# One sum for a chunk of x, both turned halves on ScalarE and one Newton chain for two in the steps without tiles

## The chip, the core and the metric

The kernel runs on one core of a Trainium2 chip. The metric is device microseconds from launch to end, as the median of several runs.

## The reference, cut to what matters

`x` is (64, 12, 224, 224). Each 16x16 patch is summed, and twelve channels are mixed into a 192 wide token. A layer of attention with a polynomial in place of the exponential follows, then a mixture of eight experts of which each token takes two.

```python
pooled = x.reshape(Bb, Cc, n, K, n, K).sum(axis=(3, 5))
h = jnp.einsum('bcij,ce->bije', pooled, channel_weights).reshape(Bb, n * n, EMBED)
h = h + attn(layernorm(h), w_qkv, w_proj, b_proj)      # attn = relu(1 + qk + qk^2/2), normalised
h = h + ffn(layernorm(h), router_w, w1, b1, w2, b2)    # top 2 of 8 experts, exact gelu
# layernorm(x) = (x - mean) / sqrt(var + 1e-5)
```

## The kernel before, in words

The 64 images go through in 16 **steps** of four images. A step has 8 blocks of 98 tokens. Its x (9.6 MB) comes in 14 **chunks** of 672 KB into seven slots of `xbuf`; each chunk is two **halves**, and a half is summed by one VectorE instruction (`P`, L1069: 21 sums of 32 numbers on each partition). After each half `s_pooled` rises by one, and SyncE reloads the slot when both halves are summed (`P` of SyncE, L490, load L469).

The work of a step has stages, each with a part on several engines. Step s+1 is pooled while step s is in its later stages:

- **S1** (in steps without tiles `T1`): TensorE mixes the sums of the next step (L866), which needs all 28 halves.
- **S2** (in steps without tiles `T2`, L1171, for step s+1): VectorE reads the mixed channels and their variance, takes 1/sqrt of it with `inverse_root` (L1127: a first guess and three Newton rounds of three instructions, each of which waits for the one before) and builds the products `phi`.
- **S3**: TensorE makes moments (L876) and turns `phi` (L802); ScalarE copies `gts` (L680) and `phiT` (L682). **S4** and **S5**: two more products (L888, L898) with ScalarE copies between them (L686, L692, L693). **S6**: TensorE makes the numerators in four quarters (L909), VectorE divides each (`rden` L1183, `att` L1185).
- **S7**: TensorE turns `att` in four pieces, the upper and the lower half of the channels for each of two groups of images (L802). ScalarE copies the upper half to `attA` (L697), VectorE the lower one to `attB` (L1190).
- **S8**: TensorE multiplies (L933 from `attA`, L934 from `attB`) in four quarters, ScalarE copies `h1s` (L705), VectorE takes statistics and the top 8 of the router (L1197, L1198).
- **S10**: VectorE gathers mean and variance `var2`, the indices of the two best and the mask. **R** (L1219): a second `inverse_root` for the rows of the experts, then `shift2` (L1222) and `gap` (L1224). **V**: ScalarE takes a tanh of `gap` (L712) and normalises the rows (L716), in its queue ahead of S3 of the next step.
- **S11**, **S9**: VectorE finishes the gates and the slots (L1230 to L1255). **Q**: GpSimd scatters the rows with 16 indirect DMAs (L608). S11 and V wait until the rows of the step before have landed.

Who does what when is written out by hand: `tiles_do` (L403) walks a list of names, and each engine runs its own handler for each name in that order. Steps 0, 1 and 2 have the list `STEP_ALONE` (L159), step 3 has `LAST` (L169), in which the first experts' tiles are prepared (G0 to G5). Those four are the steps without tiles. Steps 4 to 15 (`ORDER`) carry three tiles of 512 rows of the experts each, and a tail of tiles follows. `P` takes the halves in order, so the place of each in the list is its number:

```python
STEP_ALONE = """S3 P P P P P P P P P P P P P P P P S4 S5 P P S6.0 S6.1 P S6.2 P S6.3 S7.0 P P S7.1 P P S8.0 P S8.1 P S8.2 P P S8.3
    T1 S10 T2 R V.0 V.1 S11 V.2 V.3 S9 Q0 Q1 Q2 Q3""".split()
LAST = """S3 P P P P P P P P P P S4 S5 P P P G0 G4 S6.0 S6.1 S6.2 S6.3 S7.0 P S7.1 P P G5 G1 P S8.0 S8.1 S8.2 S8.3 S10
    R V.0 S11 V.1 V.2 S9 V.3 Q0 Q1 Q2 Q3 P P P G2 P P P P G3 P P P P""".split()
```

`mark` and `own` (L1048, L1053) count the links of VectorE's own chain; each step has 44, and the count has to come out the same whichever list is run. Seven halves of step 1 are summed in the setup (`n_early`).

Of the kernel before, what the change touches and what calls it, by code (L numbers as in the profile page):

```python
# [181 lines left out]
def vit_layer(nc, x, cw, w_qkv, w_proj, b_proj, router, w1, b1, w2, b2, consts, padids, out):  # L182
# [3 lines left out]
    with ExitStack() as ctx:  # L186
# [27 lines left out]
        var1 = sb("var1", [TOK, NT])  # L214
        rstd1 = sb("rstd1", [TOK, NT])
        newton = sb("newton", [TOK, 2, NT])
# [12 lines left out]
        var2 = sb("var2", [TOK, NT])  # L229
        rstd2 = sb("rstd2", [TOK, NT])  # L230
# [139 lines left out]
        rank_bank, lone = [2], [False]  # L370
# [214 lines left out]
        def _(pool):  # L585
# [8 lines left out]
            given("pool", "fills", nc.gpsimd.memset(rstd1[:], 1.0))  # L594
# [58 lines left out]
        def _(act):  # L653
# [388 lines left out]
        def _(dve):  # L1042
# [3 lines left out]
            pos_ = {k: 0 for k in links}  # L1046

            def mark(ins, kind="step"):  # L1048

                pos_[kind] += 1  # L1050
                return ins.then_inc(own_sem[kind], 1)
# [10 lines left out]
            def P(s, p, first=False):  # L1062
# [64 lines left out]
            def inverse_root(s, y, v):  # L1127


# [3 lines left out]
                for _ in range(3):  # L1133
                    mark(V.tensor_tensor(newton[:, 0], y, y, ALU.mult))
                    own(s)
                    mark(V.scalar_tensor_tensor(out=newton[:, 1], in0=newton[:, 0], scalar=-0.5, in1=v,
                                                op0=ALU.mult, op1=ALU.mult))
                    own(s)
                    mark(V.scalar_tensor_tensor(out=y, in0=newton[:, 1], scalar=1.5, in1=y,
                                                op0=ALU.add, op1=ALU.mult))  # L1140
                    own(s)
# [3 lines left out]
            def S2(s, round=None):  # L1145
# [11 lines left out]
                mark(V.tensor_reduce(var1[:], prod[:], AX.X, ALU.add))  # L1157
                own(round)
                mark(V.tensor_scalar(var1[:], var1[:], EPS, None, ALU.add))
                own(round)  # L1160
                inverse_root(round, rstd1[:], var1[:])
                mark(V.tensor_tensor(phi[:, :, 1:U], att_ch, bc(rstd1[:], C), ALU.mult))
# [8 lines left out]
            def T2(s):  # L1171

                before = pos_["step"]
                S2(s + 1, s)
# [26 lines left out]
            def S10(s):  # L1201
# [7 lines left out]
                V.tensor_scalar(var2[:].unsqueeze(2), mv[:, :, 1:2], EPS, None, ALU.add)  # L1209
# [9 lines left out]
            def R(s):  # L1219

                inverse_root(s, rstd2[:], var2[:])
                V.scalar_tensor_tensor(out=shift2[:].unsqueeze(2), in0=mv[:, :, 0:1], scalar=-1.0,  # L1222
                                       in1=rstd2[:].unsqueeze(2), op0=ALU.mult, op1=ALU.mult)
                V.tensor_tensor(gap[:], gap[:], rstd2[:], ALU.mult).then_inc(s_gap, 1)  # L1224
# [158 lines left out]
            def P_left(s, p):  # L1383
                if after_first(s) or p >= n_early[0]:
# [43 lines left out]
```

## Time and profile before

| | |
|---|---|
| median of 3 runs | 1357.04 us (1356.02 to 1359.77) |
| profiled execution | span 1353.8 us from its first to its last instruction; what lies outside the span is not recorded apart |
| busy | PE 91%, DVE 71%, ACT 44%, POOL 44% of the span |
| setup | 0 to about 63 us |
| steps without tiles | about 63 to 231 us |
| steps with tiles | about 231 to 1050 us |
| tail of tiles | to the end |

The page of the profile gives busy shares for the whole span and, in forty slices, when each engine was busy. The stages differ, so each is read by itself: timelines of single engines, where each line has the start, the duration, the engine, the source line, the operation and what it writes and reads, and in brackets the idle time ahead of it with what ended that.

### The profile page before, as it was taken

What the parts mean: (1) busy time and instruction counts of PE and PEld (TensorE: products, weight loads), DVE (VectorE), ACT (ScalarE), POOL (GpSimd) and SP (SyncE); (2) the same over time, 40 slices, a digit from 0 to 9 for tenths busy, and PEclk for the clock granted to TensorE, in tenths of its full rate; (3) what the DMA queues carried; (4) which work ended last, traced back from release to release, by engine and by line L of the source; (5) the groups of instructions that cost most, each with busy time, mean ns of one, the idle gap of its engine ahead of it and who ended that gap; (6) DMA issues with size and microseconds to landing.
All of it is one profiled execution on the core that took longest, in us unless ns stands there. A gap on an engine that the chain in (4) does not pass through costs nothing.

```text
span 1353.8 us, 26903 instructions
## 1 busy us (share of the span) xinstructions
PE 1228.0 (91%) x7299; PEld 1093.9 (81%) x7299; DVE 956.8 (71%) x3407; ACT 596.2 (44%) x1127; POOL 600.4 (44%) x483
## 2 busy tenths in 40 slices
PE   5867766999999999899999899999999979999997
PEld 3756655888888888788888788888888879998996
DVE  6799998787878787877787687868783523333454
ACT  1221223454545454445444354535454534544664
POOL 0104333425454454453644545464555464533433
PEclk9986556999999999898999899989999989999999
DMA  9679887767878887778786878877744655544555
GB/s 354 231 254 347 320 281 262 231 220 240 238 232 221 255 216 245 204 238 218 234 246 217 210 237 234 250 208 234 195 129 80 211 117 130 107 95 89 119 142 112
DMA packets 126551, 284.42 MB, mean 210 GB/s; under 512 B 24819, under 2 KB 70500, under 8 KB 126500
## 3 DMA queue, kind: packets, MB, share of 16 engines
q1 hardware_dynamic: 82762, 241.95, 54.5%
q0 software_dynamic: 43104, 41.25, 17.7%
q10 hardware_dynamic: 634, 0.61, 0.2%
q8 instruction: 23, 0.38, 0.1%
q14 instruction: 28, 0.23, 0.0%
HBM read 228.79 MB, written 54.95 MB: 210 GB/s over the span
## 4 chain that ended last, share of the span: by engine, by line
PE 33%; DMA 19%; DVE 17%; POOL 15%; issue 14%; ACT 1%; POOLq 1%; SPq 0%; ACTq 0%; DVEq 0%
PE ps L993 11%; DMA result<-ys,ridx 11%; PE ps L962 10%; POOL rows_d L608 8%; DMA rows_d<-rows,sloti 7%; POOL result L623 7%; DVE red L1069 6%; PE ps L802 3%; PE ps L933 2%; PE ps L934 2%; DMA w1r<-L_attn_w_qkv 1%; DVE stats L1197 1%; DVE topi L1206 1%; PE ps L1022 1%; DMA xr<-rows_d 1%
## 5 line engine op out<-in xcount | busy, mean ns | idle before, releaser
L623 POOL DMA_INDIRECT result<-ys,ridx x210 | 333.1, 1586 | 307.9 <-issue 120.4
L993 PE MATMUL ps<-w2a,hid 128*128 x2520 | 455.5, 327 | 0.0
L608 POOL DMA_INDIRECT rows_d<-rows,sloti x256 | 258.9, 1011 | 394.0 <-DMA rows_d<-rows,sloti 146.7
L993 PEld LDWEIGHTS ps<-w2a,hid 128*128 128x128 f32 x2520 | 415.4, 190 | 11.8 <-issue 0.2
L1069 DVE TENSOR_REDUCE red<-xbuf 128x21 f32<-128x672 f32 x448 | 359.2, 841 | 5.3 <-PE ps L866 2.4
L727 ACT ACTIVATE hid<-ps,b1s 128x512 f32<-128x512 f32 (+1 forms) x344 | 222.9, 654 | 239.2 <-PE ps L962 230.5
L962 PE MATMUL ps<-xh,w1h 128*128 128x512 f32 (+1 forms) x344 | 166.0, 482 | 7.9 <-DVE xl L1306 3.9
L1329 DVE TENSOR_TENSOR w1l<-w1r,w1h 128x768 fp32r<-128x768 f32 x116 | 110.3, 951 | 70.9 <-ACT w1h L739 70.3
L962 PE MATMUL ps<-xh,w1l 128*128 128x512 f32 (+1 forms) x344 | 131.5, 382 | 0.0
L962 PE MATMUL ps<-xb,w1h 128*128 128x512 f32 (+1 forms) x344 | 131.3, 382 | 0.0
L962 PE MATMUL ps<-xl,w1h 128*128 128x512 f32 (+1 forms) x344 | 131.2, 381 | 0.0
L962 PE MATMUL ps<-xb,w1l 128*128 128x512 f32 (+1 forms) x344 | 130.8, 380 | 0.0
L739 ACT CAST w1h<-w1r 128x768 fp32r<-128x768 f32 x116 | 96.2, 830 | 28.4 <-PE ps L962 28.1
L760 ACT ACTIVATE ys<-ps,gate 128x192 f32<-128x192 f32 x210 | 71.7, 423 | 73.9 <-PE ps L993 73.7
L1306 DVE TENSOR_TENSOR xl<-ps,xh 128x512 fp32r<-128x512 f32 (+1 forms) x58 | 37.1, 639 | 88.8 <-ACT xh L746 88.6
L802 PE MATMUL ps<-cst,xr 128*128 128x128 f32 (+1 forms) x428 | 67.3, 277 | 22.0 <-DMA xr<-rows_d 14.4
L962 PEld LDWEIGHTS ps<-xh,w1h 128*128 128x128 f32 x344 | 66.3, 193 | 22.2 <-issue 6.9
L746 ACT CAST xh<-ps 128x512 fp32r<-128x512 f32 (+1 forms) x58 | 31.8, 548 | 107.6 <-PE ps L802 107.5
L802 PEld LDWEIGHTS ps<-cst,xr 128*128 128x128 f32 (+1 forms) x428 | 53.8, 143 | 30.8 <-DMA xr<-rows_d 14.3
L962 PEld LDWEIGHTS ps<-xb,w1l 128*128 128x128 f32 x344 | 65.6, 191 | 13.4
L962 PEld LDWEIGHTS ps<-xh,w1l 128*128 128x128 f32 x344 | 65.8, 191 | 13.0
L962 PEld LDWEIGHTS ps<-xb,w1h 128*128 128x128 f32 x344 | 65.8, 191 | 13.1
(164 smaller groups left out, 1633.8 us busy)
## 6 DMA issues: line engine op xcount, KB each, us to landing
xbuf<-x SPq DMA_DIRECT2D x224, 672.0 KB, 5.6
w1r<-L_ffn_w SPq DMA_DIRECT2D x118, 384.0 KB, 3.7
xr<-rows_d SPq DMA_DIRECT2D x48, 402.0 KB, 3.4
result<-h1s SPq DMA_DIRECT2D x32, 294.0 KB
w2a<-L_ffn_w SPq DMA_DIRECT2D x8, 576.0 KB, 7.6
rows_d<-rows,sloti POOLq DMA_INDIRECT x256
rows_d<-pad SPq DMA_DIRECT2D x9, 402.0 KB, 4.6
result<-ys,ridx POOLq DMA_INDIRECT x210, 4.9
```

The costliest lines, as they stand in the source:

```text
L608: pool.indirect_dma_start(rows_d, bass.IndirectOffsetOnAxis(ap=sloti[:, k * NT + t:k * NT + t + 1], axis=0), rows[:, t, :], None).then_inc ...
L623: pool.indirect_dma_start(out, bass.IndirectOffsetOnAxis(ap=ridx[:, b, n:n + 1], axis=0), ys[:, b, n, :], None, compute_op=ALU.add).then_i ...
L727: nc.scalar.activation(hid[:, m % 3, 0:128 * g], ps[:, bank(b, f"M{m}"), 0:128 * g], ACT.Gelu, bias=b1s[:, b, m:m + 1]).then_inc(s_hT, 1)
L739: copy(w1h[:, :, cols], w1r[:, nb, q]).then_inc(s_w1h, 1)
L746: copy(xh[:, nb, 0:128 * g], ps[:, bank(b, "X0"), 0:128 * g]).then_inc(s_xa, 1)
L760: nc.scalar.activation(ys[:, b, i, :], yout(g, b, i), ACT.Copy, scale=gate[:, b, i:i + 1]).then_inc(s_ys, TP // g)
L802: return nc.tensor.transpose(dst, src, ident[0:n, 0:n])
L962: last = mm(ps[:, bank(b, f"M{m}"), 0:128 * g], w, r, start=i == 0, stop=i == len(parts) - 1)
L993: last = mm(yout(g, b, n), hid[:, m % 3, cols], w, start=False, stop=m == MC - 1 and n % 2 == 1)
L1069: V.tensor_reduce(red[:, p * SUMS:(p + 1) * SUMS], xbuf[:, k % XSLOTS, h], AX.X, ALU.add).then_inc(s_pooled, 1)
L1306: V.tensor_tensor(xl[:, nb, 0:128 * g], ps[:, bank(b, "X0"), 0:128 * g], xh[:, nb, 0:128 * g].bitcast(F32), ALU.subtract).then_inc(s_xd, 1)
L1329: V.tensor_tensor(w1l[:, :, cols], w1r[:, nb, q], w1h[:, :, cols].bitcast(F32), ALU.subtract).then_inc(s_w1l, 1)
```

## The change

It has three parts, all for the steps without tiles.

1. `P` gets a form `whole`: one VectorE instruction sums both halves of a chunk (42 sums of 32 numbers) and raises `s_pooled` by two. It stands where the even half stood, and the odd half's place stays empty. This holds for the halves from 8 on in step 0 and for all in steps 1 to 3.
2. In S7 the copy of `attB` goes from VectorE to ScalarE, behind the copy of `attA` of the same group. VectorE keeps its wait for the turn.
3. `var1` and `var2`, `rstd1` and `rstd2` lie side by side. In steps 0 to 2 `T2` takes both roots at once, with ten instructions of 16 columns instead of 8, and `R` has no chain of its own; it raises the counter of the links by ten. Step 3 and the steps with tiles keep two chains.

```diff
             lone[0] = not with_tiles and not last
+            early[0] = not with_tiles
...
                 copy(attA[:, g * IPS * TOK:(g + 1) * IPS * TOK],
                      ps[0:KA, TURN[2 * g], 0:IPS * TOK]).then_inc(s_tA, 1)
+                if early[0]:
+                    act.wait_ge(s_turn, s * 4 + 2 * g + 2)
+                    copy(attB[:, g * IPS * TOK:(g + 1) * IPS * TOK],
+                         ps[0:KB, TURN[2 * g + 1], 0:IPS * TOK]).then_inc(s_tB, 1)
...
-                V.tensor_reduce(red[:, p * SUMS:(p + 1) * SUMS], xbuf[:, k % XSLOTS, h], AX.X,
-                                ALU.add).then_inc(s_pooled, 1)
+                if whole:
+                    V.tensor_reduce(red[:, p * SUMS:(p + HALVES) * SUMS].rearrange("p (h n) -> p h n", h=HALVES),
+                                    xbuf[:, k % XSLOTS], AX.X, ALU.add).then_inc(s_pooled, HALVES)
+                else:
+                    V.tensor_reduce(red[:, p * SUMS:(p + 1) * SUMS], xbuf[:, k % XSLOTS, h], AX.X,
+                                    ALU.add).then_inc(s_pooled, 1)
...
-            def inverse_root(s, y, v):
+            def inverse_root(s, which):
+                y = roots[:, which].rearrange("p k t -> p (k t)")
+                v = vars_[:, which].rearrange("p k t -> p (k t)")
...
-                inverse_root(round, rstd1[:], var1[:])
+                inverse_root(round, slice(0, 2) if both else slice(0, 1))
...
-                S2(s + 1, s)
+                S2(s + 1, s, both=True)
...
                 dve.wait_ge(s_turn, s * 4 + 2 * g + 2)
+                if early[0]:
+                    return
                 V.tensor_copy(attB[:, g * IPS * TOK:(g + 1) * IPS * TOK],
...
             def R(s):
-                inverse_root(s, rstd2[:], var2[:])
+                if not lone[0]:
+                    inverse_root(s, slice(1, 2))
...
+                if lone[0]:
+                    mark(shifts, n=ROOT)
...
             def P_left(s, p):
-                if after_first(s) or p >= n_early[0]:
+                if early[0] and (after_first(s) or p > n_early[0]):
+                    if p % HALVES == 0:
+                        P(s, p, whole=True)
+                elif after_first(s) or p >= n_early[0]:
                     P(s, p)
```

## Rows read from the trace of the kernel before

**Rows 1.** The page: busy time and share of the span of each engine.

```profile
PE 1228.0 (91%) x7299; PEld 1093.9 (81%) x7299; DVE 956.8 (71%) x3407; ACT 596.2 (44%) x1127; POOL 600.4 (44%) x483
```

**Rows 2.** Windows: start:end, length, busy of five engines, PE clock, DMA share, GB/s.

```profile
95.50:137.20 41.70, 28.58 (x141) 24.51 (x141) 38.94 (x134) 9.43 (x20) 15.26 (x16) 0.58 0.84 306
137.20:180.20 43.00, 29.53 (x141) 25.26 (x141) 38.98 (x133) 9.43 (x20) 15.20 (x16) 0.58 0.85 308
...
240.00:1000.00 760.00, 728.65 (x4392) 648.54 (x4392) 603.80 (x2120) 365.70 (x676) 371.09 (x296) 0.98 0.79 226
...
600.00:640.00 40.00, 38.15 (x209) 34.23 (x209) 28.17 (x107) 18.61 (x38) 19.09 (x13) 0.91 0.84 221
```

**Rows 3.** Groups of VectorE from 95 to 236 us: count, busy us, mean ns.

```profile
L1069 DVE TENSOR_REDUCE red<-xbuf 128x21 f32<-128x672 f32 x84 | 65.6, 843 | 0.3 <-issue 0.3
...
L1157 DVE TENSOR_REDUCE var<-prod 98x8 f32<-98x96 f32 x3 | 0.8, 253 | 0.1
```

**Rows 4.** Timeline of VectorE, second root of step 0 to its pooling.

```profile
95.48 0.16 DVE L1131 TENSOR_SCALAR rstd<-var 98x8 int32<-98x8 int32 x1
...
97.48 0.17 DVE L1222 SCALAR_TENSOR_TENSOR shift<-mv,rstd 98x8 f32<-98x8 f32 x1
...
100.01 13.77 DVE L1069 TENSOR_REDUCE red<-xbuf 128x21 f32<-128x672 f32 x18
```

**Rows 5.** Timeline of ScalarE in step 1.

```profile
97.87 3.60 ACT L716 ACTIVATE rows<-h1s,shift,rstd 98x192 f32<-98x192 f32 x8
...
101.72 0.80 ACT L682 COPY phiT<-ps 91x784 f32<-91x784 f32 x1
...
119.82 0.49 ACT L697 COPY attA<-ps 103x392 f32<-103x392 f32 x1 [1.35 <-PE ps L802]
```

**Rows 6.** Timeline of TensorE in step 1.

```profile
98.16 1.61 PE L802 MATMUL ps<-cst,phi 98*91 98x98 f32 x8
...
111.51 5.76 PE L909 MATMUL ps<-us,phiT 91*98 91x204 f32 x16 [0.98 <-ACT us L693]
...
118.77 1.66 PE L802 MATMUL ps<-cst,att 98*103 98x98 f32 x8 [0.17 <-DVE att L1185]
120.23 0.88 PE L933 MATMUL ps<-resA,attA 103*98 103x200 f32 x2
```

**Rows 7.** Timeline of VectorE in step 1, from the numerators to the statistics.

```profile
113.69 0.30 DVE L1183 RECIPROCAL rden<-ps 98x24 f32<-98x24 f32 x1
...
120.64 0.56 DVE L1190 COPY attB<-ps 102x392 f32<-102x392 f32 x1
121.11 1.60 DVE L1069 TENSOR_REDUCE red<-xbuf 128x21 f32<-128x672 f32 x2
123.69 0.36 DVE L1197 BATCH_NORM_STATS2 stats<-h1s 98x6 f32<-98x192 f32 x1 [0.98 <-ACT h1s L705]
```

**Rows 8.** Timeline of TensorE in step 2.

```profile
160.74 1.66 PE L802 MATMUL ps<-cst,att 98*103 98x98 f32 x8 [0.44 <-DVE att L1185]
162.20 0.88 PE L933 MATMUL ps<-resA,attA 103*98 103x200 f32 x2
...
166.86 0.71 PE L934 MATMUL ps<-resB,attB 102*98 102x200 f32 x2
167.41 0.50 PE L933 MATMUL ps<-resA,attA 103*98 103x200 f32 x2
```

**Rows 9.** Timeline of VectorE in step 3.

```profile
212.88 0.36 DVE L1197 BATCH_NORM_STATS2 stats<-h1s 98x6 f32<-98x192 f32 x1 [0.60 <-ACT h1s L705]
...
220.93 2.36 DVE L1069 TENSOR_REDUCE red<-xbuf 128x21 f32<-128x672 f32 x3
223.21 0.68 DVE L1306 TENSOR_TENSOR xl<-ps,xh 128x512 fp32r<-128x512 f32 x1
...
225.04 6.16 DVE L1069 TENSOR_REDUCE red<-xbuf 128x21 f32<-128x672 f32 x8
```

**Rows 10.** Timelines at the end of step 3: ScalarE's `xh`, TensorE's S1.

```profile
222.46 0.59 ACT L746 CAST xh<-ps 128x512 fp32r<-128x512 f32 x1
...
231.25 1.51 PE L866 MATMUL ps<-mixg,red 128*98 128x96 f32 x12 [1.94 <-DVE red L1069]
```

**Rows 11.** Timelines of GpSimd and VectorE around the scatter of step 0.

```profile
131.34 0.95 POOL L608 DMA_INDIRECT rows_d<-rows,sloti  x1 [0.30 <-issue]
...
139.35 0.17 DVE L1230 CAST rows<-ids 98x8 int32<-98x8 f32 x1
```

More of the change, by code:

```diff
@@ L213, in vit_layer @@
         prod = sb("prod", [TOK, NT, C])
-        var1 = sb("var1", [TOK, NT])
-        rstd1 = sb("rstd1", [TOK, NT])
-        newton = sb("newton", [TOK, 2, NT])
+        vars_ = sb("vars", [TOK, 2, NT])
+        roots = sb("roots", [TOK, 2, NT])
+        var1, var2 = vars_[:, 0], vars_[:, 1]
+        rstd1, rstd2 = roots[:, 0], roots[:, 1]
+        newton = sb("newton", [TOK, 2, 2 * NT])
         phi = sb("phi", [TOK, NT, NF])
@@ L369, in vit_layer @@
         at_end = [False]
-        rank_bank, lone = [2], [False]
+        rank_bank, lone, early = [2], [False], [False]
         def groups(j):
@@ L593, in _ @@
             nc.gpsimd.memset(b2t[:], 0.0)
-            given("pool", "fills", nc.gpsimd.memset(rstd1[:], 1.0))
+            given("pool", "fills", nc.gpsimd.memset(roots[:], 1.0))
             pool.wait_ge(d_w, 16 * 9)
@@ L1046, in _, with mark @@
             pos_ = {k: 0 for k in links}
-            def mark(ins, kind="step"):
-                pos_[kind] += 1
-                return ins.then_inc(own_sem[kind], 1)
+            ROOT = 10
+            def mark(ins, kind="step", n=1):
+                pos_[kind] += n
+                return ins.then_inc(own_sem[kind], n)
             def own(i, kind="step", alone=False):
@@ L1060, in bc, with P @@
                 return ap.unsqueeze(len(ap.shape)).to_broadcast(list(ap.shape) + [n])
-            def P(s, p, first=False):
+            def P(s, p, first=False, whole=False):
                 k, h = p // HALVES, p % HALVES
@@ L1125, in _ @@
             given("dve", "b2", V.tensor_copy(b2s[:, 2], b2f[:, 0]))
-            def inverse_root(s, y, v):
+            def inverse_root(s, which):
+                y = roots[:, which].rearrange("p k t -> p (k t)")
+                v = vars_[:, which].rearrange("p k t -> p (k t)")
+                n = y.shape[1]
+                squares, halves = newton[:, 0, 0:n], newton[:, 1, 0:n]
                 mark(V.tensor_scalar(y.bitcast(I32), v.bitcast(I32), -0.5, float(0x5f3759df), ALU.mult, ALU.add))
@@ L1133, in inverse_root @@
                 for _ in range(3):
-                    mark(V.tensor_tensor(newton[:, 0], y, y, ALU.mult))
+                    mark(V.tensor_tensor(squares, y, y, ALU.mult))
                     own(s)
-                    mark(V.scalar_tensor_tensor(out=newton[:, 1], in0=newton[:, 0], scalar=-0.5, in1=v,
+                    mark(V.scalar_tensor_tensor(out=halves, in0=squares, scalar=-0.5, in1=v,
                                                 op0=ALU.mult, op1=ALU.mult))
                     own(s)
-                    mark(V.scalar_tensor_tensor(out=y, in0=newton[:, 1], scalar=1.5, in1=y,
+                    mark(V.scalar_tensor_tensor(out=y, in0=halves, scalar=1.5, in1=y,
                                                 op0=ALU.add, op1=ALU.mult))
@@ L1219, in R @@
             def R(s):
-                inverse_root(s, rstd2[:], var2[:])
-                V.scalar_tensor_tensor(out=shift2[:].unsqueeze(2), in0=mv[:, :, 0:1], scalar=-1.0,
-                                       in1=rstd2[:].unsqueeze(2), op0=ALU.mult, op1=ALU.mult)
-                V.tensor_tensor(gap[:], gap[:], rstd2[:], ALU.mult).then_inc(s_gap, 1)
+                if not lone[0]:
+                    inverse_root(s, slice(1, 2))
+                shifts = V.scalar_tensor_tensor(out=shift2[:].unsqueeze(2), in0=mv[:, :, 0:1], scalar=-1.0,
+                                                in1=rstd2.unsqueeze(2), op0=ALU.mult, op1=ALU.mult)
+                if lone[0]:
+                    mark(shifts, n=ROOT)
+                V.tensor_tensor(gap[:], gap[:], rstd2, ALU.mult).then_inc(s_gap, 1)
             def S11(s):
```

12 lines of the change are left out of this document (5 added, 7 removed).

## The prediction

> **What bounds the kernel now.** I begin with the page. TensorE is busy 91% of the span and VectorE 71% [rows 1], which would say that an edit of VectorE's work is worth little. The windows say otherwise of the stage that the edit touches. In steps 1 and 2 VectorE is busy 38.9 of 41.7 and 39.0 of 43.0 us and TensorE, at a mean clock of 0.58, only 28.6 and 29.5; from 240 to 1000 us TensorE is busy 728.65 of 760 us [rows 2]. So the steps with tiles go at TensorE's pace and the steps without tiles at a loop that runs mostly through VectorE. What is saved there moves all that follows to the left.
>
> The loop is read in the timelines of step 1. VectorE ends `phi`, and behind it stands the second root, from 95.48 to the start of `shift2` at 97.48 [rows 4]. Only then can ScalarE take the tanh and normalise rows, 97.87 plus 3.60, and behind these in its queue are the copies of S3 for the next step, `phiT` at 101.72 [rows 5], although TensorE has turned it by 98.16 + 1.61 = 99.77 [rows 6]. S4, S5 and the numerators (111.51) hang on that. At the same time VectorE sums 18 halves, 100.01 to 113.78 [rows 4], and comes to the first numerator at 113.69 [rows 7]; the first quarter of the sixteen products that take 5.76 us is ready at 111.51 + 1.44 = 112.95 [rows 6]. The two arms of the loop, VectorE's pooling and the ScalarE/TensorE arm, thus differ by 0.7 us only. After the numerators TensorE and ScalarE lead: VectorE idles 0.98 us for `h1s` [rows 7].
>
> **The change part by part.**
>
> *The joined root.* The second chain goes: 97.48 − 95.48 = 2.00 us [rows 4], in three steps. The joined chain has 8 more columns in ten instructions. The slope of VectorE's sums is (843 − 253)/(672 − 96) = 1.02 ns for a column [rows 3], so 80 ns more ahead of `phi`. On VectorE's arm pooling starts 2.0 us sooner after `phi`. On the other arm rows are normalised 2.0 us sooner and end at 97.87 + 3.60 − 2.0 = 99.47; `phiT` could then start at 99.8, and TensorE has turned it at 99.77, so nearly all of the 2.0 arrives; I take 1.9. Net 1.9 − 0.1 = 1.8 a step, **5.4 us** in three. What is late next on this arm is TensorE's turn of `phi`, 0.1 us behind: a longer cut would have been lost there. In step 3 `R` keeps its chain, so nothing there.
>
> *The whole chunk.* Eighteen halves take 13.77 us with the last of 0.84 running out, so (13.77 − 0.84)/17 = 0.76 us from one to the next [rows 4]. 672 columns at 1.02 ns are 0.69, which leaves about 0.07 us for each instruction. One of 1344 columns doesn't occur in the trace. Its bounds are 1.52 us (nothing saved) and 1.37 (no fixed part at all); I take 2 x 0.76 − 0.07 = 1.45, since a single instruction keeps one fixed part, and rows of either length lie on that line. There are 10 such pairs in step 0 and 14 in each of three, 52 x 0.07 = 3.6 us of VectorE. On the path is little of it. The 9 chunks ahead of the numerators bring VectorE's arm 2.0 + 0.6 us forward where the other comes 1.9 forward; with its slack of 0.7 the other arm then decides, just. Between S8.0 and S8.3 there are two chunks, 0.14 us in each of three steps, **0.4 us**. In step 3 half 17 moves ahead of S8.0 and costs nothing: 0.7 us more there against 0.5 from the copy that has gone and 0.6 of idle time at the last `h1s` [rows 9]. Behind S9 there were 3 + 8 halves, and now 1 + 4 chunks. The three give way to one (1.45 for 2.28), but `xl` then waits for `xh`, which ended at 223.05 [rows 10] against 223.21 [rows 9], so 0.1 is won and not 0.8; the eight give 4 x 0.07 = 0.3. **0.4 us**. TensorE's mix starts 0.1 us behind the last sum, at 231.25 [rows 10], and releases the steps with tiles.
>
> The places move too. In S6 the chunk stands whole between the second and third quarter, so the third `att` is 0.7 us later and the fourth 0.07 earlier. TensorE still has the fourth numerator and the first turns to do until then. It costs nothing while the numerators' 5.76 us end after that, which holds in steps 1 and 2. SyncE reloads a slot when a chunk's second half is done, which is 0.07 us sooner or earlier still; no load waits longer, and in the stage VectorE idled 0.3 us in all ahead of its sums, none of it for a load [rows 3].
>
> *The copies on ScalarE.* VectorE loses two `attB` copies a step, 121.11 − 120.64 = 0.47 us each [rows 7], 3.8 us in four steps. I cost this at nothing: behind them VectorE idles 0.98 us for `h1s` [rows 7], and will idle some 2 us. ScalarE gets two copies of 392 columns; the nearest row is `attA` with 0.49 us, and it idled 1.35 us ahead of that [rows 5]. Behind the copy of `attB` of group 0 stands only `attA` of group 1, which S8.1 needs 2.7 us after S8.0 starts. In step 3 ScalarE's casts of `w1` come 0.4 us later, ahead of a `w1l` that VectorE reaches 0.5 us sooner; the slack up to `h1s` is over 1 us. Cover gone, a copy costs 0.4 to 0.5 us a step.
> The Trainium skill speaks against this part: "Trainium Architecture — The Big Picture", "The five engines, in one table", says that ScalarE is not for simple arithmetic and that VectorE is up to about three times faster for each element. The rows of the same width read 0.49 us on ScalarE and 0.56 on VectorE [rows 5, 7], so they don't bear it out for a copy from PSUM. At three times, an estimate from that page, a copy would take 1.5 us and the second one of a group would reach into S8.1, at about 1 us a step.
>
> *Gaps closed.* TensorE waited 0.17 us in step 1 and 0.44 in step 2 for the fourth `att` [rows 6, 8]. VectorE's arm comes forward by 2.6 and the other by 1.9, so these go: **0.6 us**.
>
> *A landing.* S11 and V of step 1 wait until the rows of step 0 have landed. Their last indirect DMA starts at 131.34, and VectorE passes the wait at 139.35 [rows 11]. Between them lie 8.0 us, 0.95 for the DMA's issue and the rest for its landing and what margin there is. The scatter starts 2.0 us sooner, the wait comes 2.0 + 1.8 sooner (the cuts of steps 0 and 1), so the margin shrinks by 1.8. Bounds 0 and 1 us; I take 0.1, as step 2's margin is larger.
>
> *The clock.* TensorE runs these stages at half clock until deep in S8: the products come every 0.67 us and every 0.34 after the rise to 2.4 GHz. In step 2 seven pairs are slow (162.20 to 166.86) [rows 8]; in step 1 the rise comes after four. The engine had then worked nearly without a gap from the numerators on. If the rise keeps its time while the products start 2 us sooner, three more pairs are slow, and VectorE's chunk between the quarters hides about half of it; if it comes earlier in step 2, 0.9 us of idle time go. Bounds −1 and +2 us over the stage, in my sum 0.
>
> Sum: 5.4 + 0.4 + 0.4 + 0.6 − 0.1 = 6.7 us. The span of the profiled execution would go from 1353.8 to 1347.1; it is 3.2 us under the median of the runs, and the same offset gives 1357.0 − 6.7 = **1350.3 us**. It passes through if the steps with tiles take the shift whole. They do the same instructions in the same order on the same data, so nothing in the code holds them to a time.
>
> **The rivals.**
> 1. *The gain is cut or given back.* TensorE at half clock keeps the slow pairs (1 us), S11 waits for the landing (1 us), and an S6 or S7 order gives 0.5 us a step; or the steps with tiles lose a little. For it: the two arms are only 0.7 us apart and a third, TensorE's turn, 0.1 us. Against: each single part is small. Half the gain, 3.4 us: 1353.6. Chance 0.2.
> 2. *VectorE alone sets the stage.* Then all its work counts: 3 x 1.9 + 3.6 + 3.8 = 13.1 us, 1343.9. For it its 93%; against it the 0.98 us for `h1s` [rows 7]. Chance 0.03.
> 3. *Slower.* The mechanism is TensorE's clock in the steps with tiles. The stretch from 600 to 640 us has a mean clock of 0.91 [rows 2], which is 7.2 us at 1.2 GHz and up to 3.6 us of work not done in them; such a fall stands in few of the stretches, since from 240 to 1000 us the mean is 0.98, about four falls' worth. Shifted arrivals can put a short wait of TensorE where it lets the clock fall. From two more falls on (2 x 3.6 = 7.2) the gain is gone; with three more, one in every fourth of the twelve steps with tiles, the time is 1350.3 + 10.8 = 1361.1. Chance 0.04. The Trainium skill ("TensorE: Matmul & The Clock Gate", "Part 1: The HAM clock gate") says that the engine is slow by default and that activity releases it, by which a fall needs TensorE to idle; the stretches with 0.91 do have less work done. It would leave this chance as low as it is.
> 4. *It doesn't do what it says.* The instruction of 1344 columns takes as long as two. Then the 0.4 + 0.3 go and the pooling arm comes 2.0 forward, still ahead of the other: 1351.1, inside the forecast.
>
> **How the numbers follow.** Forecast 0.72, rivals 0.2, 0.03 and 0.04, and 0.01 for the rest. The forecast with its bounds is 1348 to 1352.5 (clock, landing, chunk). Runs of one kernel spread over 3.7 us. To hold 8 in 10 the range reaches into rival 1 and a little towards rival 2: 1346.5 to 1354.5. A measurement can tell from no change about 0.3%, that is 4.1 us, so faster means under 1352.9. That holds in nearly all of the forecast, in rival 2 and in a quarter of rival 1: 0.76. Same 0.19, slower 0.05.
>
> **What would show it.** From the end of `phi` to the next, steps 1 and 2 take 41.7 and 43.0 us; I expect about 39.7 and 40.7, and step 0 hardly changed. ScalarE's `rows` start 0.4 us after `phi`, not 2.4. The chunk's instruction has a duration near 1.53 us and follows its like every 1.45. VectorE's idle time ahead of the first statistics grows from 1 to about 2 us, which is where the copies went. TensorE's mix of step 4 starts near 224.5, not 231.25. From there on the timelines should be the old ones, shifted. I am wrong if `phi` to `phi` shrinks by under 1.3 us (an arm that I took for slack decides), or by over 3, or if the distance from TensorE's mix of step 4 to the end, 1122 us, changes by more than 2 us.

## The result and the profile after

| | before | after |
|---|---|---|
| median of 13 runs each | 1356.76 us (1352.57 to 1363.85) | 1365.01 us (1357.17 to 1367.87) |
| ratio to before, 95% interval | | 1.005 [1.0032, 1.0068] |
| profiled span | 1353.8 us | 1363.5 us (its execution took 1365.31) |
| mix of step 4 starts | 231.25 us | 227.58 us |
| from there to the mix of step 15 | 771.8 us | 786.6 us |
| from there to the end | 350.7 us | 349.4 us |

The change makes the kernel 0.5% slower where I forecast 0.5% faster. (The ratios here and below are of undisturbed runs of both kernels on one chip, and so can differ a little from the quotient of the medians.) The last three lines of the table split the span: the part that was edited gained 3.7 us, the part in which nothing was edited lost 14.8, and the tail gained 1.3. Sum +9.8 by the rounded numbers, against 9.7 in the spans.

First the page, busy time of each engine and the queue that fetches instructions, whose columns are packets, MB and share. The first line answers [rows 1].

```profile
PE 1238.0 (91%) x7299; PEld 1098.3 (81%) x7299; DVE 945.8 (69%) x3317; ACT 600.4 (44%) x1135; POOL 598.9 (44%) x483
...
q14 instruction: 78, 0.64, 0.1%
```

VectorE did 11 us less. The line of the queue read `q14 instruction: 28, 0.23, 0.0%` before: fifty packets more. That is a row of which I had made nothing.

Next the windows, for [rows 2] (a step's slow stage, and the steps with tiles).

```profile
100.00:140.00 40.00, 28.65 (x136) 24.55 (x137) 34.86 (x106) 9.44 (x21) 14.35 (x16) 0.59 0.91 332
...
240.00:1000.00 760.00, 720.91 (x4297) 637.51 (x4296) 589.63 (x2070) 355.13 (x657) 364.53 (x288) 0.97 0.78 225
```

In the same 760 us TensorE got 7.7 us less done. To compare equal work (4455 products in both) I take the windows from the mix of step 4 to the mix of step 15, before and after:

```profile
231.25:1003.07 771.82, 740.47 (x4455) 659.23 (x4456) 612.78 (x2157) 368.00 (x681) 376.53 (x300) 0.98 0.78 226
227.58:1014.14 786.56, 746.78 (x4455) 660.52 (x4456) 612.22 (x2157) 368.23 (x681) 377.16 (x300) 0.97 0.76 223
```

Of the 14.8 us TensorE is idle for 8.4 more (31.4 and 39.8) and busy 6.3 more for the same products. The two clocks are 0.976 and 0.974 to a third digit, which is under 2 us of it; I have no cause for the rest of the busy time. The idle time by itself proves little, since the kernel with all parts undone, below, idles 39.6 us there too. What TensorE waited for, from 240 to 1000 us (who waited for whom, us in total, times, longest):

```profile
PE ps L967 <- DVE xl L1325: 19.6, 17, 1.8
PE ps L881 <- DVE phi L1179: 7.7, 10, 1.8
```

The trace of before has no wait of TensorE for `phi` in these steps; its longest sum is 18.6 us for `att`, which is 4.8 after. So the waits moved, and one in every turn is new. And `phi` is made late because VectorE stands still ahead of it. Its waits from 240 to 1040 us:

```profile
DVE rden L1197 <- PE ps L914: 54.9, 12, 6.4
DVE vars L1173 <- issue: 30.7, 10, 4.2
DVE xl L1325 <- ACT xh L751: 24.3, 11, 2.2
DVE avail L1283 <- issue: 14.1, 10, 2.0
```

"Issue" is time in which the engine waited for nothing that the profile shows. The trace of before has neither of the two rows. Both are in ten turns, once a turn, of the loop of the steps with tiles. (The loop is walked eleven times, for steps 4 to 14, so VectorE jumps back ten times.) Here is one turn's start, VectorE's timeline, after:

```profile
368.97 0.17 DVE L1283 COPY avail<-base 128x8 f32<-128x8 f32 x1 [1.02 <-issue]
369.78 0.26 DVE L1166 COPY att<-ps 98x96 f32<-98x96 f32 x1 [0.63 <-PE ps L871]
370.07 0.25 DVE L1168 TENSOR_TENSOR prod<-att,ps 98x96 f32<-98x96 f32 x1
370.36 0.25 DVE L1171 TENSOR_REDUCE vars<-prod 98x8 f32<-98x96 f32 x1
373.29 0.17 DVE L1173 TENSOR_SCALAR vars<-vars 98x8 f32<-98x8 f32 x1 [2.68 <-issue]
```

and the same place before:

```profile
367.21 0.15 DVE L1264 COPY avail<-base 128x8 f32<-128x8 f32 x1
369.09 0.26 DVE L1152 COPY att<-ps 98x96 f32<-98x96 f32 x1 [1.74 <-PE ps L866]
369.38 0.25 DVE L1154 TENSOR_TENSOR prod<-att,ps 98x96 f32<-98x96 f32 x1
369.67 0.25 DVE L1157 TENSOR_REDUCE var<-prod 98x8 f32<-98x96 f32 x1
369.96 0.17 DVE L1159 TENSOR_SCALAR var<-var 98x8 f32<-98x8 f32 x1
```

Before, the step ahead of the root follows its predecessor at once. After, VectorE stands still for 2.7 us between two instructions of a few hundred nanoseconds of which the second needs only the first. One turn of the steps with tiles is one pass of a loop in VectorE's code, and `avail` is the first instruction behind the jump to its start, where the other 1.0 us of idle time lies, there still partly hidden by the wait for the mix.

Last the steps without tiles, VectorE and ScalarE from the second root of step 0 on, for [rows 4, 5, 7]:

```profile
95.70 0.16 DVE L1239 SCALAR_TENSOR_TENSOR shift<-mv,roots 98x8 f32<-98x8 f32 x1
...
98.29 13.23 DVE L1076 TENSOR_REDUCE red<-xbuf 128x42 f32<-128x1344 f32 x9
111.54 0.31 DVE L1197 RECIPROCAL rden<-ps 98x24 f32<-98x24 f32 x1
...
122.08 0.36 DVE L1213 BATCH_NORM_STATS2 stats<-h1s 98x6 f32<-98x192 f32 x1 [1.64 <-ACT h1s L710]
```

```profile
96.08 3.60 ACT L721 ACTIVATE rows<-h1s,shift,roots 98x192 f32<-98x192 f32 x8
100.03 0.81 ACT L683 COPY phiT<-ps 91x784 f32<-91x784 f32 x1
...
117.05 0.49 ACT L702 COPY attB<-ps 102x392 f32<-102x392 f32 x1 [0.27 <-PE ps L807]
118.83 0.49 ACT L702 COPY attB<-ps 102x392 f32<-102x392 f32 x1 [0.17 <-PE ps L807]
```

and TensorE's products of step 1, for [rows 6]:

```profile
118.58 0.88 PE L938 MATMUL ps<-resA,attA 103*98 103x200 f32 x2
...
122.58 0.88 PE L938 MATMUL ps<-resA,attA 103*98 103x200 f32 x2
123.25 0.78 PE L939 MATMUL ps<-resB,attB 102*98 102x200 f32 x2
```

`rows` starts 1.8 us sooner, the numerators' first division 2.1 sooner, the products 1.65 sooner. All of this came as worked out. But the mix of step 2 (L871) starts at 128.22 instead of 128.84: from 87.39, step 1 took 40.8 us instead of 41.6, and the next two 41.0 for 43.0 and 58.4 for 59.4. TensorE waited for VectorE's sums ahead of that mix both times.

### The profile page after: what moved, and what is told of

Its sections match the earlier page's. It is cut to its first block, busy times and chain, and to the rows that moved or that the text cites. A ratio compares the mean times of both kernels' runs of the same rounds, so it can differ in the third digit from the quotient of the medians.

```text
span 1363.5 us, 26853 instructions
## 1 busy us (share of the span) xinstructions
PE 1238.0 (91%) x7299; PEld 1098.3 (81%) x7299; DVE 945.8 (69%) x3317; ACT 600.4 (44%) x1135; POOL 598.9 (44%) x483
## 4 chain that ended last, share of the span: by engine, by line
PE 49%; DVE 32%; issue 12%; ACT 3%; DMA 2%; POOL 1%; DVEq 0%; ACTq 0%; POOLq 0%; SPq 0%
PE ps L998 17%; PE ps L967 16%; DVE red L1079 8%; PE ps L807 3%; PE ps L903 2%; PE ps L893 2%; DVE stats L1213 2%; PE ps L914 2%; DVE w1l L1348 2%; DVE red L1076 2%; DVE phi L1179 2%; DVE topi L1222 1%; PE ps L938 1%; PE ps L939 1%; DVE xl L1325 1%
## 5 line engine op out<-in xcount | busy, mean ns | idle before, releaser
L998 PE MATMUL ps<-w2a,hid 128*128 x2520 | 463.1, 331 | 0.0
L998 PEld LDWEIGHTS ps<-w2a,hid 128*128 128x128 f32 x2520 | 423.4, 194 | 12.4 <-issue 0.2
L1079 DVE TENSOR_REDUCE red<-xbuf 128x21 f32<-128x672 f32 x344 | 277.7, 841 | 5.0 <-PE ps L871 2.4
L1076 DVE TENSOR_REDUCE red<-xbuf 128x42 f32<-128x1344 f32 x52 | 77.8, 1543 | 3.2 <-PE ps L807 2.6
L967 PEld LDWEIGHTS ps<-xb,w1l 128*128 128x128 f32 x344 | 65.9, 192 | 13.4
```

The lines of the kernel that those rows point to most:

```text
L967: last = mm(ps[:, bank(b, f"M{m}"), 0:128 * g], w, r, start=i == 0, stop=i == len(parts) - 1)
L998: last = mm(yout(g, b, n), hid[:, m % 3, cols], w, start=False, stop=m == MC - 1 and n % 2 == 1)
L1076: V.tensor_reduce(red[:, p * SUMS:(p + HALVES) * SUMS].rearrange("p (h n) -> p h n", h=HALVES), xbuf[:, k % XSLOTS], AX.X, ALU.add).then_i ...
```

## The experiments

**The theory** after the traces: it is the place of the loop in VectorE's code. The list of instructions ahead of the loop of the steps with tiles was 36 shorter (541 instead of 577 in the built programs), while the loop itself kept its length. If code is fetched in blocks, the loop begins at another place of a block, covers one more, and is fetched anew in every turn. **The rival**: the work in the steps with tiles arrives shifted by 3.7 us against x and the experts' DMAs and the tiles' order, and loses by that. A second one is that a part of the change does harm by what it computes.

The tool for all of them is padding that does nothing: increments of a semaphore on VectorE, put where it idles about 5 us at the start of the program for its first load.

```diff
+            for _ in range(36):
+                dve.sem_inc(s_waits, 1)
             dve.wait_ge(d_cst, 16)
```

**The change with 36, 12 and 4 increments in front.** With 36 the loop is where it was before.

> The changed kernel with 36 short semaphore instructions put in front of VectorE's stream, where it idles 5 us for its first load. VectorE's list before the loop of the steps with tiles is 36 instructions shorter in the changed kernel; this gives the loop its old place. Theory P (the place of the loop in VectorE's instruction stream makes it refetch code each turn): the idle time of VectorE without a releaser at the start of each step with tiles (30.7 + 14.1 us in all) goes, the instruction packets between 320 and 960 us go from some 50 to none, and the time is 1352.5 +- 2.5, 12 us under the changed kernel. Theory C (the earlier start shifts the phase of TensorE's clock and of the DMA queues in the loop): nothing of it goes, 1363 to 1366.

> The same with 12 instructions. The stall of the changed kernel stands about 11 instructions behind the start of the loop, so by theory P the border of a block of code lies there; 12 more in front move the loop's start over the border and the loop lies in one block less: no stalls, 1352.5 +- 2.5, as with 36. Theory C: 1363 to 1366. If only the exact old place were good, this one would be as slow as the changed kernel.

> The same with 4 instructions. By theory P the border is now about 7 instructions behind the loop's start instead of 11: the stall moves from ahead of L1173 to ahead of the TENSOR_TENSOR prod (L1168) or the reduce L1171 behind it, its size stays near 3 us a step and the time stays near 1363. Theory C has no stall that moves with the count; 1363 to 1366 too. So the place of the stall decides, not the time.

**The kernel before with 220.** Here none of the change's parts is in the code.

> The kernel before with 220 such instructions in front, 256 less the 36, which puts the loop where the changed kernel has it if code is fetched in blocks of 256 instructions. Nothing else is changed; up to 3 us may be lost at the start. Theory P: VectorE's idle time without a releaser appears (some 4 us a step), about 50 more instruction packets, and from TensorE's mix of step 4 to that of step 15 the time grows from 772 to about 786 us; in all 1367 to 1372. Theory C: the distance stays near 772 and the time at 1357 to 1360.

| on one chip, before 1356.83 us | median us | ratio [95%] | mix of step 4 | mix 4 to mix 15 | q14 packets |
|---|---|---|---|---|---|
| change + 36 | 1352.81 | 0.9969 [0.9943, 0.9994] | 227.55 | 771.7 | 28 |
| change + 12 | 1349.77 | 0.9955 [0.9928, 0.9982] | 227.37 | 764.8 | 28 |
| change + 4 | 1370.57 | 1.0101 [1.0072, 1.013] | 227.83 | 792.6 | 78 |
| before + 220 | 1386.33 | 1.0226 [1.0199, 1.0254] | 244.86 | 785.5 | 80 |

The shift against the DMAs is the same in the first three (227.4 to 227.8), and the loss is there in one and gone in two. That ends the first rival. The distance itself scatters: in one profile each it is 762 to 776 us in the twelve kernels without the extra packets and 778 to 802 in the six with them. The two ranges don't touch, but a difference of a few us within one of them means nothing. The timeline of VectorE at the loop's start, with 12 and then with 4:

```profile
362.04 0.15 DVE L1285 COPY avail<-base 128x8 f32<-128x8 f32 x1
363.94 0.26 DVE L1168 COPY att<-ps 98x96 f32<-98x96 f32 x1 [1.75 <-PE ps L871]
```

```profile
366.61 0.17 DVE L1285 COPY avail<-base 128x8 f32<-128x8 f32 x1 [1.22 <-issue]
367.21 0.26 DVE L1168 COPY att<-ps 98x96 f32<-98x96 f32 x1 [0.42 <-PE ps L871]
370.47 0.25 DVE L1170 TENSOR_TENSOR prod<-att,ps 98x96 f32<-98x96 f32 x1 [3.00 <-issue]
```

With four more instructions in front the second stall comes earlier in the turn, ahead of `prod` and no longer ahead of the step behind `vars`, as a fixed border in the code requires. In the kernel before with 220 it stands ahead of `var` again, and the distance is 785.5 us: the loss is there without the change. Its start was a miss. I expected up to 3 us for the 220, but VectorE's first instruction starts at 21.99 us and not at 5.15, and the mix of step 4 comes 13.6 us later. Up to 36 of them are hidden (5.22).

**The parts alone**, each also a place of its own. In the built programs the chunk alone takes one instruction away ahead of the loop, since a wait stays where each sum or copy was; the copies alone take one too, the joined root alone takes 30, and all three together take 36. In the first kernel R keeps its chain and `attB` is copied by VectorE, in the second sums are by halves and R keeps its chain, in the third sums are by halves and VectorE copies `attB`; the fourth is the third with 30 increments.

```diff
# chunk alone, and copies alone
-                S2(s + 1, s, both=True)
+                S2(s + 1, s)
# copies alone, and root alone
-                if early[0] and (after_first(s) or p > n_early[0]):
+                if False:
```

> Only the whole chunk (part 1); the copies stay on VectorE and the roots stay two. VectorE's list before the loop is one instruction shorter than before, so theory P (place of the loop) expects no stall of code in the loop. In the steps without tiles the sums of a chunk follow each other every 1.47 us; the two arms of the loop stay where they are but for 0.1 us a step, so TensorE's mix of step 4 comes at 230.5 +- 0.4 (231.25 before). Time 1356 +- 2.5. Rival V (VectorE's work counts in full in these steps): 3.4 us, the mix at 227.8.

> Only the copies of attB on ScalarE (part 2). One instruction shorter as well: theory P expects no stall. VectorE's work falls by 3.8 us, but it waits for h1s behind it; the mix of step 4 at 231.0 +- 0.4, time 1356.5 +- 2.5. Rival V: the mix at 227.5.

> Only the joined root (part 3), 30 instructions shorter, which by theory P puts the start of the loop 5 instructions ahead of a border of a code block: the stall is back, ahead of one of the three first instructions on att and prod in each step, and from mix 4 to mix 15 the time is 785 to 793 us instead of 772. The steps without tiles gain about 3 us (mix of step 4 at 228 to 228.5), the total is 1363 to 1370. If the stall comes from the chunk or the copies and not from the count, n_alone shows none and takes 1353.

> The joined root alone with 30 short semaphore instructions in VectorE's first idle time, which gives the loop its old place. Theory P: no stall, mix of step 4 at 228 to 228.5, mix 4 to mix 15 back at 765 to 773, time 1353 +- 2.5; nearly the whole gain of the full change with the place restored, since the root is the only part on the arm that bounds.

| on one chip, before 1361.99 us | median us | ratio [95%] | mix of step 4 | mix 4 to mix 15 | q14 packets |
|---|---|---|---|---|---|
| chunk alone | 1359.77 | 0.9989 [0.9951, 1.0026] | 233.72 | 772.9 | 28 |
| copies alone | 1361.65 | 1.0015 [0.9978, 1.0052] | 234.89 | 771.0 | 28 |
| root alone | 1384.46 | 1.0172 [1.0103, 1.024] | 228.65 | 801.9 | 78 |
| root alone + 30 | 1357.84 | 0.998 [0.9945, 1.0016] | 228.39 | 770.5 | 28 |

Two expectations missed here: the mix of step 4 came 3.2 us later than I had for the chunk alone and 3.9 later for the copies alone. Their repeats below, on another chip, have it at 230.54 and 231.29. So this time scatters by some 3 us from chip to chip, and only kernels of one chip are compared in it.

The root alone, the part that I had as the best, is the one that loses: 1.7% slower. Its stalls are the largest of all; the waits of VectorE from 240 to 1040 us and one turn's start:

```profile
DVE att L1166 <- issue: 47.5, 10, 5.4
```

```profile
372.17 0.17 DVE L1281 COPY avail<-base 128x8 f32<-128x8 f32 x1 [1.39 <-issue]
376.79 0.26 DVE L1166 COPY att<-ps 98x96 f32<-98x96 f32 x1 [4.46 <-issue]
```

With 30 increments all of it is gone, and its steps without tiles keep what the root brings (228.39 against 233.72 and 234.89 of the other parts, on this chip).

**Control and repeats.** All three parts undone in the text of the changed kernel, chunk and copies alone again, and the change with 12 again, on a third chip.

> The changed file with all three parts undone: the instructions of the kernel before in the same places. It gives the stage without tiles on the same chip as the single parts. Both theories: 1357, mix of step 4 at 231 to 235, no stall in the loop; ratio to before 1.000 +- 0.002.

> The whole chunk alone, again, beside the control on the same chip. On the arm that bounds it is worth 0.1 us a step: mix of step 4 at 0.3 to 1.0 us ahead of the control's. Rival V, VectorE's work counts in full: 3.4 us ahead. Rival T, the earlier arrival only adds slow products at half clock: within 0.3 or behind.

> The copies alone, again, beside the control. Mix of step 4 within 0.5 us of the control's; rival V 3.8 us ahead.

> The full change with 12 short instructions in front, again, beside the control: mix of step 4 ahead of the control's by 3.7 to 4.5 us as on the first chip (227.4 against 231.25), and the total about 1350 where the control has 1357; no stall of code. The joined root alone was at 228.4, so whole chunk and copies together are worth 1 us here.

| on one chip, before 1359.05 us | median us | ratio [95%] | mix of step 4 | mix 4 to mix 15 |
|---|---|---|---|---|
| all parts undone | 1358.88 | 1.0007 [0.9978, 1.0036] | 230.84 | 776.3 |
| chunk alone | 1355.75 | 0.997 [0.9945, 0.9995] | 230.54 | 768.0 |
| copies alone | 1359.69 | 1.0014 [0.9986, 1.0042] | 231.29 | 766.6 |
| change + 12 | 1352.93 | 0.995 [0.9933, 0.9967] | 226.02 | 769.7 |

In the steps without tiles the chunk is worth 230.84 − 230.54 = 0.3 us, the copies −0.4 (nothing, at the spread of one profile each), and all three with the root 4.8. The ratio of the chunk alone is a bare 0.3% under 1 here and not on the chip before; I don't build on it.

**Where the borders are, TensorE kept warm, and the change without its copies.** The first puts 92 increments into the kernel before. By the Trainium skill ("Runtime: NRT & Kernel Launch", "Instruction fetch mechanics") blocks are of 256 instructions, by which this loop would cross no border that it didn't cross before. If borders come every 128, it begins just where the change put it. The second adds to the change with 12 products without use on TensorE in the steps without tiles: two behind T1, four behind S9, three behind S3, one behind S4 and S5, so that it enters the numerators at work.

```diff
+            def fill(n):
+                for _ in range(n):
+                    mm(ps[:, 7, 0:384], ident, cst[:, 0:384], start=True, stop=True)
```

> The kernel before with 92 short instructions in front of VectorE's stream (128 less 36). If code came in blocks of 128 instructions, this would put the loop where the changed kernel has it, with stalls and from mix 4 to mix 15 about 786 us. If in blocks of 256, the loop ends at 25 + 92 + some 305 instructions, short of the second border at 512: no stall, 765 to 775 us. The instructions themselves cost about 1 us at the start, since VectorE idles 5 us there. Expected: no stall, 1356 to 1362. It also tells that instructions put in front don't slow the loop by their number.

> The full change with 12 instructions in front, and products without use on TensorE in its idle gaps of the steps without tiles: 384 columns of a constant into a bank that is free, two behind the mix, four behind the ranks, three behind S3, one behind S4 and S5 each. Theory T (the half clock holds the gain back: the slow pairs of S8 eat what arrives sooner): the granted clock of 100 to 220 us rises from about 0.6 to near 1, VectorE's idle times for h1s and the numerators (1.64, 0.46, 0.60 us in step 1) shrink, the steps without tiles take 37.5 to 39.5 us where they took 40.8, and the mix of step 4 comes at 218 to 223 instead of 227.4. If TensorE's arm isn't held by the clock, or the products without use delay what follows them, it stays at 227 to 229.

> Joined root and whole chunk without the copies, with 12 instructions in front. If the copies on ScalarE are free or worth nothing, the mix of step 4 comes within 0.5 us of the full change's 226 to 227.4. If ScalarE's copy holds S8 back, it comes sooner by 0.5 us or more; if taking them off VectorE helps, later by as much. Time 1350 to 1354, no stall.

| on one chip, before 1352.4 us | median us | ratio [95%] | mix of step 4 | mix 4 to mix 15 | q14 packets |
|---|---|---|---|---|---|
| before + 92 | 1382.03 | 1.0239 [1.0194, 1.0285] | 233.85 | 790.9 | 79 |
| change + 12, products without use | 1345.53 | 0.9953 [0.9929, 0.9977] | 228.33 | 762.1 | 28 |
| root and chunk, + 12, no copies | 1344.44 | 0.9948 [0.9918, 0.9978] | 226.72 | 763.7 | 28 |

The 92 were a miss, and the most telling run: the kernel before, with nothing but empty instructions in front, is 2.4% slower (30 us between the medians, of which the later start of VectorE, 9.76 us for 5.15, can be 5) and stalls at the change's two places. The timeline of one turn:

```profile
375.29 0.17 DVE L1266 COPY avail<-base 128x8 f32<-128x8 f32 x1 [1.43 <-issue]
...
379.57 0.17 DVE L1161 TENSOR_SCALAR var<-var 98x8 f32<-98x8 f32 x1 [3.05 <-issue]
```

92 is 128 − 36. 220 is 92 + 128. So the pattern repeats every 128 instructions. A packet on the queue (0.64 MB in 78) carries 8 KB; if that is one such block, an instruction takes 64 bytes. From 320 to 940 us the trace of before has no packet on this queue, and after the change it has 42:

```profile
q14 instruction: 42, 0.34, 0.1%
```

The profile has a second queue of this kind, on which no edit of VectorE changed anything (`q8 instruction: 23, 0.38, 0.1%`). Its 23 packets of 0.38 MB are of 16 KB, so the size isn't the same on both.

The warm kernel missed what it was for. The windows of the step from 100 to 140 us and the products of step 1:

```profile
100.00:140.00 40.00, 33.42 (x165) 25.00 (x164) 34.42 (x105) 8.90 (x20) 14.45 (x16) 0.79 0.92 333
```

```profile
119.10 0.88 PE L938 MATMUL ps<-resA,attA 103*98 103x200 f32 x2
...
123.10 0.82 PE L938 MATMUL ps<-resA,attA 103*98 103x200 f32 x2
123.75 0.50 PE L939 MATMUL ps<-resB,attB 102*98 102x200 f32 x2
```

The mean clock went from 0.59 to 0.79, but it had fallen again by the time S8 began (0.50 from 118 to 123 us), and seven groups of products were slow, as in the change with 12 alone. I had expected the mix of step 4 at 218 to 223; it came at 228.33. Nothing follows on what a warm S8 would give. The kernel without the copies is as good as the one with them (0.9948 and 0.9953).

**The border further behind the loop's start.** The change with 101 increments begins its loop so that it still covers four blocks, but with the next border 38 instructions behind its start and not 11.

> The changed kernel with 101 short instructions in front. With blocks of 128 the loop of some 306 instructions starts at place 90 of a block and lies in four blocks, as in the changed kernel (place 117), but the first border is 38 instructions behind the start and not 11. If four blocks alone are what costs, instruction packets (some 50 from 320 to 960 us) and both stalls are there and mix 4 to mix 15 takes 784 to 788 us. If the load of the second block hides behind the instructions ahead of the border, the packets are there and the stall of 1.4 us at the jump too, but that of 3 us shrinks below 1 or goes, and the distance is 770 to 781. The start costs about 1 us (mix of step 4 at 228 to 229).

| on one chip, before 1351.22 us | median us | ratio [95%] | mix of step 4 | mix 4 to mix 15 | q14 packets |
|---|---|---|---|---|---|
| change + 101 | 1360.66 | 1.0057 [1.0021, 1.0093] | 229.24 | 777.7 | 78 |

```profile
370.53 0.17 DVE L1285 COPY avail<-base 128x8 f32<-128x8 f32 x1 [1.69 <-issue]
370.93 0.26 DVE L1168 COPY att<-ps 98x96 f32<-98x96 f32 x1 [0.22 <-DVE avail L1285]
...
371.80 0.17 DVE L1175 TENSOR_SCALAR vars<-vars 98x8 f32<-98x8 f32 x1
372.00 0.17 DVE L1147 TENSOR_SCALAR roots<-vars 98x8 int32<-98x8 int32 x1
```

The blocks are still fetched anew each turn (78 packets). The stall at the jump grew (21.1 us in ten turns for 14.1), and the one behind it is gone. In the profile most of the lost distance went with it (777.7 us, where the change has 786.6), but the median is no better: the ratio to before is 1.0057, and that of the change on its chip was 1.005. A mix of step 4 that comes 1.7 us later (229.24) is a part of that; the rest stays open. (The profile also names 10.3 us ahead of `rden` in three turns "issue"; the kernel with the chunk alone, which fetches nothing anew, has 6.9 such in two, so that isn't the border.)

The places side by side. The start of the loop is counted in VectorE's list with the loads that the compiler adds, modulo 128; the loop is about 306 long. Which place counts as 0 was fitted to one stall and then held for the others. The blocks are counted from this.

| kernel | loop starts at | blocks | to the next border | stall ahead of an instruction between jump and border, mean us |
|---|---|---|---|---|
| change + 12 | 1 | 3 | | none |
| root and chunk + 12 | 6 | 3 | | none |
| chunk alone, copies alone | 24 | 3 | | none |
| before, change + 36, root alone + 30, all undone | 25 | 3 | | none |
| change + 101 | 90 | 4 | 38 | none |
| change, before + 92, before + 220 | 117 | 4 | 11 | 3.1, 3.3, 2.8 |
| change + 4 | 121 | 4 | 7 | 3.8 |
| root alone | 123 | 4 | 5 | 4.75 |

## Why the prediction was wrong

**The step that failed** is its last: "They do the same instructions in the same order on the same data, so nothing in the code holds them to a time." The sentence is true of what the instructions do and left out where they lie. The steps with tiles lost 14.8 us. The change took 36 instructions away ahead of the loop, and the joined root by itself takes 30. The loop then lay in four blocks of 128 and not in three, and four are not kept from one turn to the next: 50 packets more, in ten turns five each. VectorE waits 1.4 us for the first behind the jump and 3.1 us at the border 11 instructions later, 4.5 a turn and 44.8 in ten. Some 15 of these reach the end in the profile. Much of the rest was hidden: VectorE had waited 19.4 us for the mix ahead of `att` before and waits 4.7 after, and TensorE waits only 7.7 us for `phi`. Put in or out by empty instructions alone, the loss came and went in both kernels. That is shown. On one chip the change with 12 is at 0.9955 and with 4 at 1.0101. How the wait of VectorE passes on to each later stage was not followed further.

"Instruction fetch mechanics" in the Trainium skill's "Runtime: NRT & Kernel Launch" says that a taken branch whose target isn't in the window of two pages forces a fetch before the engine goes on. On the stall at the jump the traces agree, with 1.4 us a turn. By its blocks of 256 instructions the kernel with 92 would not have changed; it lost 2.4%, and a loop over three blocks of 128 was not fetched anew, so here the measurement decides.

My rival for *slower* had TensorE's clock as its mechanism, with three falls more at 3.6 us each. Over equal work the clock went from 0.976 to 0.974, which is under 2 us, so it was at most a small part. The sign of a possible loss was in the range (0.05), its cause wasn't among the rivals.

**The steps without tiles**, forecast 6.7 us, got 3.7. How many us sooner than before TensorE starts each thing, in one profile each:

| step | mix | numerators | first products of S8 | last pair of S8 | next mix |
|---|---|---|---|---|---|
| 1 | −0.14 | 1.69 | 1.65 | 0.41 | 0.62 |
| 2 | 0.62 | 2.33 | 2.56 | 2.54 | 2.66 |
| 3 | 2.66 | 4.49 | 3.90 | 3.22 | 3.67 |

The columns give the terms of my sum one by one:

- *The joined root*, 5.4. Right. From mix to numerators 1.83 + 1.71 + 1.83 = 5.4 us are won. `rows` start 0.4 us after `phi`, as I wrote, and `phiT` 1.7 sooner.
- *The whole chunk*. Its instruction takes 1543 ns (forecast 1.53) and they follow each other every (13.23 − 1.54)/8 = 1.46 us (forecast 1.45). Its value on the path, 0.4 + 0.4 forecast: from the last pair to the next mix 0.21 + 0.12 + 0.45 = 0.8 us, of which 0.45 behind S9. Alone against the control it gave 0.3, which one profile each can't tell from it.
- *The copies*, nothing. Right: 0.49 us each, VectorE's idle time ahead of the first statistics from 0.98 to 1.64 us (I wrote about 2), and neither alone nor taken out do they move anything beyond the scatter.
- *Gaps closed*, 0.6. The two waits are gone from the trace, but from the numerators to the products only −0.04 + 0.23 = 0.2 us are won in steps 1 and 2. In step 1 the turns took no longer before, with their gap, than now without it.
- *The numerators of step 3*, not in my sum: 0.6 us are lost. They start 4.5 us sooner, but TensorE then waits for the first `att`:

```profile
196.85 1.68 PE L914 MATMUL ps<-us,phiT 91*98 91x204 f32 x4 [0.70 <-DVE att L1199]
```

  There VectorE chooses the first experts' tiles (G0) ahead of the division, and comes to it at 195.91 for 199.81, 3.9 us sooner. In this step its arm decides; I had read the arms in step 1 only.
- *The clock*, 0 with bounds −1 and +2. This is the mis-sized term of this part: 1.24 + 0.02 + 0.68 = 1.9 us are lost between the first and the last pair of S8. In step 1 the products start 1.65 us sooner, but the rise to 2.4 GHz comes at about 123.9 us against 122.9, so eight groups are slow instead of four and the last pair starts only 0.4 us sooner. In step 3 the products start 3.9 us sooner and the last pair 3.2. In step 2 it is seven to eight both times [rows 8]. I had weighed a rise that keeps its time and one that comes earlier, and took nothing between them; in step 1 it came later. That the groups are slow, and that the time goes there, the rows show. Why the rise comes when it does I can't say: the run that was to hold the clock up didn't.
- *The landing*, 0.1. No wait for it shows.

From the end of `phi` to the next, steps 1 and 2 took 41.1 and 40.9 us, where I had 39.7 and 40.7. So step 1 shrank by 0.6 only, under the 1.3 that I had set as a sign of being wrong: there the clock took back what the root gave.

Had the loop kept its place, the change with 36 would have been the result: 0.9969, which on 1356.8 is 1352.6, inside the range and 2.3 us over the forecast. With 12 it would be 0.9955 or 1350.7 us, nearly the forecast itself, and that is in part luck: its edited part won 3.9 us and not 6.7, and the rest is a shorter distance in the steps with tiles (764.8 for 771.8 in the profiles), which is inside the scatter. In my own test "the distance from TensorE's mix of step 4 to the end changes by more than 2 us" the error is named; it changed by 13.4.

**A better version.** The change with 12 increments ahead of VectorE's first wait is 0.45 and 0.5% faster than before on two chips, and by these ratios about 1% faster than the change. Root and chunk without the copies, with 12, are as good (0.9948).

## What to carry to other kernels

When an edit changes the number of instructions ahead of a loop (or in it), it moves the loop against the borders of its code, and an engine that jumps back each turn can pay some us at places that nobody edited. Look at the packets of the instruction queue and at idle time of an engine with no releaser just behind a jump: both stand in the profile and both were quiet before. And before an edit is judged by its total, put empty instructions in front of it where the engine is idle; it took 12 of them to turn +0.5% into −0.5%. Where the idle time is too short for them they cost time of their own: behind 220 of them the mix of step 4 came 13.6 us later.

## What the runs showed of the hardware

- VectorE's code has a border every 128 instructions, and the packets that come with it are of 8 KB. A loop of about 306 instructions that lies in three such blocks is not fetched anew; in four, five packets a turn are (places 1 to 25 and 90 to 123; none in between was run).
- The price in a turn is 1.3 to 2.1 us at the jump (means of six kernels), and at the border behind it 4.75, 3.8 and 2.8 to 3.3 us where that stands 5, 7 and 11 instructions further, nothing at 38. What of it reaches the end is less: 14.8 us of 44.8 in the change.
- An increment of a semaphore costs VectorE some 95 ns where it isn't hidden: its first instruction starts at 9.76 us behind 92 of them and at 21.99 behind 220.
- Products without use between the stages raised TensorE's mean clock from 0.59 to 0.79 (100 to 140 us) and did not keep it up to the stage for which they were meant.
